# Two groups of rows finished inside the attention's first three steps, their rows kept in the weights' landing buffer

## The reference

```python
x = L0_attn_hidden_states                                   # [2, 2048, 256]
x = x + _layernorm(_L0_attn_ref(_layernorm(x), ...))        # part 1: local, compressed and selected attention
x = x + _layernorm(_L0_ffn_ref(_layernorm(x), ...))         # part 2: two transformer layers

# part 1, the end of it (win: 64 rows to a window, half overlapping)
combined = concatenate([comp_out * gates[..., 0:1], sel_out * gates[..., 1:2], win_out * gates[..., 2:3]], -1)
out = combined @ Wo + bo
out = out * 0.5 + hidden_states * 0.5
mu, var = out.mean(-1), out.var(-1)
return (out - mu) * rsqrt(var + 1e-06)

# part 2, one layer: x [2, 2048, 256]; 8 heads of 64; windows of 128 rows that look one window back
h = shift_token(x)                       # second half of the columns comes from the row before
q, k, v = split(h @ wqkv, 3)             # then l2norm, scales, rotary embedding
o = local_attention(q, k, v)
x = x + o @ wo
h = layernorm(shift_token(x)) * lg + lb
a, g = split(h @ w1 + b1, 2)
x = x + (a * gelu(g)) @ w2 + b2
```

## Time and profile before

| | |
|---|---|
| time, median of 3 runs | 1545.32 us (1541.97 to 1547.23) |
| the profiled execution | 1544.35 us, of which the span is 1542.2 us |
| instructions | 35890 |
| busy share: PE, DVE, ACT, POOL | 93%, 75%, 68%, 51% |
| the local stage's last matmuls end | at about 248 us |
| attention of layer 0 | about 261 to 680 us |

### The profile page before, as it was taken

One profiled execution on the slowest core, in us unless ns is written; L12 is line 12 of the kernel. 1 busy time (PEld: TensorE's weight loads), 2 busy tenths in 40 slices (PEclk: granted clock), 3 DMA queues, 4 the chain that ended last, 5 costly groups with the idle time before them and its releaser, 6 DMA issues.

```text
span 1542.2 us, 35890 instructions
## 1 busy us (share of the span) xinstructions
PE 1433.8 (93%) x10499; PEld 1195.9 (78%) x10499; DVE 1151.2 (75%) x3067; ACT 1047.3 (68%) x2678; POOL 791.9 (51%) x971
## 2 busy tenths in 40 slices
PE   8899995899999999959999979999999996899996
PEld 6458883688888888857888868888888885687775
DVE  6763686888888888856556488888888886656564
ACT  4222576788888888854545468888888886355553
POOL 4003266666666666623323556666666663334442
PEclk9999997999999999989999999999999998899998
DMA  5000323200000000002000020000000000111211
GB/s 182 1 1 18 136 94 113 59 7 6 5 5 7 5 5 5 5 8 94 16 23 16 19 66 6 7 5 5 5 5 5 5 5 8 32 37 32 63 33 60
DMA packets 59314, 46.63 MB, mean 30 GB/s; under 512 B 13662, under 2 KB 56002, under 8 KB 59234
## 3 DMA queue, kind: packets, MB, share of 16 engines
q1 hardware_dynamic: 59234, 45.65, 10.0%
HBM read 26.24 MB, written 8.39 MB: 22 GB/s over the span
## 4 chain that ended last, share of the span: by engine, by line
PE 76%; DVE 9%; ACT 6%; issue 4%; POOL 2%; DMA 1%; DVEq 0%; SPq 0%; ACTq 0%; POOLq 0%
PE bank L1993 8%; PE bank L2033 8%; PE bank L1934 7%; PE bank L1952 6%; PE bank L1855 6%; PE bank L1857 6%; PE bank L1856 6%; PE bank L1881 4%; PE bank L2107 3%; PE bank L2108 3%; PE bank L2109 3%; PE bank L1708 2%; DVE act_full L2813 2%; PE bank L1784 1%; PE bank L1717 1%
## 5 line engine op out<-in xcount | busy, mean ns | idle before, releaser
L1286 ACT ACTIVATE prob<-prob,neg_max 128x256 f32<-128x256 f32 x512 | 255.6, 507 | 1.2 <-DVE neg_max L2609 1.1
L850 POOL TENSOR_TENSOR rnorm<-sumsq,neg_half 128x8 f32<-128x8 f32 x128 | 213.5, 1668 | 23.4 <-POOL sumsq L847 22.7
L861 POOL TENSOR_TENSOR qk_cs<-qk_cs 128x512 f32<-128x512 f32 x128 | 181.7, 1420 | 56.0 <-DVE qk_cs L2489 55.7
L1855 PE MATMUL bank<-wqkv_hi,hT_hi 128*128 128x512 f32 x384 | 164.4, 428 | 19.3 <-DVE hT_lo L2471 19.3
L2489 DVE TENSOR_TENSOR qk_cs<-bank,rope 128x1024 f32<-128x1024 f32 x128 | 156.0, 1219 | 0.6 <-ACT qk_sq L1208 0.6
L2107 PE MATMUL bank<-h_hi,w_hi 128*128 128x512 f32 (+1 forms) x352 | 140.8, 400 | 14.5 <-POOL h_lo L909 14.4
L1856 PE MATMUL bank<-wqkv_lo,hT_hi 128*128 128x512 f32 x384 | 152.6, 397 | 0.0
L1857 PE MATMUL bank<-wqkv_hi,hT_lo 128*128 128x512 f32 x384 | 152.5, 397 | 0.0
L1439 ACT ACTIVATE act_hi<-act_full 128x512 fp32r<-128x512 f32 x96 | 60.7, 632 | 135.2 <-DVE act_full L2813 135.2
L1993 PE MATMUL bank<-ident,prob 128*128 128x128 f32 x1024 | 139.5, 280 | 5.1 <-DVE x_sb L2663 4.5
L2813 DVE SCALAR_TENSOR_TENSOR act_full<-bank,b_sb,gelu_sb 128x512 f32<-128x512 f32 x96 | 71.7, 746 | 93.1 <-ACT gelu_sb L1433 58.3
(11 more groups left out here) (291 smaller groups left out, 4166.8 us busy)
## 6 DMA issues: line engine op xcount, KB each, us to landing
x_sb<-in_L_attn_hidden_states SPq DMA_DIRECT2D x8, 512.0 KB, 7.6
x_in<-in_L_attn_hidden_states SPq DMA_DIRECT2D x8, 512.0 KB, 4.9
x_scratch<-x_in SPq DMA_DIRECT2D x8, 512.0 KB, 3.1
f_x<-x_scratch SPq DMA_DIRECT2D x8, 512.0 KB, 4.7
out<-f_y SPq DMA_DIRECT2D x8, 512.0 KB, 3.2
raw<-in_L_ffn_w SPq DMA_DIRECT2D x6, 640.0 KB
hs<-x_sb SPq DMA_DIRECT2D x16, 224.0 KB
hs<-x_sb SPq DMA_DIRECT2D x64, 56.0 KB
```

The lines of the kernel that those rows point to most:

```text
L850: pool.tensor_tensor(rnorm[:, part * HEADS:(part + 1) * HEADS], sumsq[:, which * HEADS:(which + 1) * HEADS], neg_half[:, 0:HEADS], ALU.pow ...
L861: pool.tensor_tensor(z, z, other[:, :, ::-1, :], ALU.add).then_inc(z_ready[which], 1)
L1286: act.activation(prob[:, h], prob[:, h], ACT.Exp, bias=neg_max[:, h:h + 1], scale=-1.0, accum_out=psums[:, h:h + 1]).then_inc(exped, 1)
L1855: pe.matmul(bank[:, to], hT_hi[:, c], wqkv_hi[:, c, cols], start=(c == 0), stop=False)
```

## The change

Groups 6 and 7 no longer use `x0_in`. Their rows are loaded into the first 2048 columns of `raw`, under the new name `x0_late`, after `ffn_split` has reached `FIRST`; `x0_of(g)` picks the place. The small tiles `f_bst1`, `f_mv1`, `f_r`, `f_shift` move out of the bytes that the attention uses. With that, the last part of the chain of groups 6 and 7 moves into the attention's steps, and ACT and DVE wait only for groups 0 to 5 before the first squares:

```diff
+        x0_late = raw[:].rearrange("p a n -> p (a n)")[:, 0:2 * GB * D].rearrange("p (a b d) -> p a b d", a=2, b=GB)
...
+        def x0_of(g):
+
+            return x0_late[:, g - (NG - 2)] if g >= NG - 2 else x0_in[:, g % 4]
...
                 sp.wait_ge(x1_stored, 16 * (g - 1))
-                sp.dma_start(x0_in[:, g % 4], group_of(x0_b, g)).then_inc(x0_loaded[g % 4], 16)
+                if g >= NG - 2:
+                    sp.wait_ge(ffn_split, FIRST)
+                    settle(sp)
+                sp.dma_start(x0_of(g), group_of(x0_b, g)).then_inc(x0_loaded[g % 4], 16)
...
@@ POOL: the local loop @@
-            for G in range(1, NG + 3):
+            for G in range(1, NG + 1):
...
@@ POOL: the attention's steps @@
                 for n in range(6):
                     step(n, n % 2)
+                    if not lay and n == 1:
+                        x1_scales(NG - 2)
+                        x1_scales(NG - 1)
...
             def first_hi():

                 act.wait_ge(hT_ps, 1)
                 act.wait_ge(x1_stored, 16 * 5)
+                act.wait_ge(x_made, GB * 5)
...
@@ ACT: the local loop @@
-            for n in range(NB + 18):
+            for n in range(NB + 6):
...
-                if n == NB + 12:
-                    first_hi()
                 if r < 2 and 0 <= n - 16 < NB:
                     b = (n - 16) // GB * GB + 2 * r
                     norm_x1(b)
                     norm_x1(b + 1)
+                if n == NB + 1:
+                    first_hi()
...
-                    act.wait_ge(x_made, NB)
-                    act.wait_ge(x1_stored, 16 * NG)
+                    act.wait_ge(x_made, NB - 2 * GB)
+                    act.wait_ge(x1_stored, 16 * (NG - 2))
...
@@ ACT: step 1, before kT, kT_lo and v_sb are cleared @@
+                    else:
+                        act.wait_ge(x1_made, NG)
...
@@ ACT: the attention's steps @@
                 for n in range(6):
                     step(n, n % 2)
+                    if not lay and n in (1, 2):
+                        for b in range(NB + (n - 3) * GB, NB + (n - 2) * GB):
+                            norm_x1(b)
...
@@ DVE: the local loop @@
-            for n in range(NB + 18):
+            for n in range(NB + 4):
...
@@ DVE: step 1, ahead of k_lo @@
+                        if type(n) is int and n == 1:
+                            if lay:
+                                add_up(lay * NG - 1, NG - 1)
+                            else:
+                                for b in range(NB - GB, NB):
+                                    x1_moments(b)
+                                    x1_aggregate(b)
...
                 if not lay:
                     lo(0, ahead=True)
-                    dve.wait_ge(x_made, NB)
-                    dve.wait_ge(x1_stored, 16 * NG)
+                    make_x1(NG - 1)
+                    x1_moments(NB - GB - 1)
+                    x1_aggregate(NB - GB - 1)
+                    dve.wait_ge(x_made, NB - 2 * GB)
+                    dve.wait_ge(x1_stored, 16 * (NG - 2))
```

More of the change, by code:

```diff
@@ L173, in build @@
         n_shift = place("n_shift", [P, GB])
+        f_bst1 = place("f_bst1", [P, 2, 6])
+        f_mv1 = place("f_mv1", [P, 2, GB, 2])
+        f_r = place("f_r", [P, 2, GB])
+        f_shift = place("f_shift", [P, 2, GB])
         base[0] = work_base
@@ L206, in build @@
         m_shift = place("m_shift", [P, 2, GB])
-        f_bst1 = place("f_bst1", [P, 2, 6])
-        f_mv1 = place("f_mv1", [P, 2, GB, 2])
-        f_r = place("f_r", [P, 2, GB])
-        f_shift = place("f_shift", [P, 2, GB])
+        place("spare", [P, 44])
         kTw = place("kTw", [P, 2, DC, UT])
@@ L554, in store_x1 @@
                     settle(sp)
-                sp.dma_start(group_of(x1_dram, g), x0_in[:, g % 4]).then_inc(x1_stored, 16)
+                sp.dma_start(group_of(x1_dram, g), x0_of(g)).then_inc(x1_stored, 16)
             def move_group(g):
@@ L759, in make_x1 @@
                 pool.wait_ge(x0_loaded[g % 4], LOCAL_X0 + 16 * (g // 4 + 1))
-                pool.tensor_tensor(x0_in[:, g % 4], x0_in[:, g % 4], xs_st[:], ALU.add).then_inc(x1_made, 1)
+                pool.tensor_tensor(x0_of(g), x0_of(g), xs_st[:], ALU.add).then_inc(x1_made, 1)
             def x1_scales(g):
@@ L1131, in norm_x1 @@
                 act.wait_ge(x1_root, g + 1)
-                act.activation(x_sb[:, b, :], x0_in[:, g % 4, r], ACT.Identity, bias=f_shift[:, g % 2, r:r + 1],
+                act.activation(x_sb[:, b, :], x0_of(g)[:, r], ACT.Identity, bias=f_shift[:, g % 2, r:r + 1],
                                scale=f_r[:, g % 2, r:r + 1]).then_inc(x_made, 1)
@@ L2405, in make_x1 @@
                 dve.wait_ge(x0_loaded[g % 4], LOCAL_X0 + 16 * (g // 4 + 1))
-                dve.tensor_tensor(x0_in[:, g % 4], x0_in[:, g % 4], xs_st[:], ALU.add).then_inc(x1_made, 1)
+                dve.tensor_tensor(x0_of(g), x0_of(g), xs_st[:], ALU.add).then_inc(x1_made, 1)
             def x1_moments(b):
                 dve.wait_ge(x1_made, b // GB + 1)
-                dve.bn_stats(f_bst1[:, b % 2], x0_in[:, b // GB % 4, b % GB]).then_inc(x1_stats, 1)
+                dve.bn_stats(f_bst1[:, b % 2], x0_of(b // GB)[:, b % GB]).then_inc(x1_stats, 1)
             def x1_aggregate(b):
@@ L2688, in step @@
                     if live(n, 1):
-                        if type(n) is int and n == 1 and lay:
-                            add_up(lay * NG - 1, NG - 1)
+                        if type(n) is int and n == 1:
[5 more added lines that the diff above has]
+                                    x1_aggregate(b)
                         k_lo(n - 1, 1 - i)
```

## The result

| | before | after |
|---|---|---|
| median, us | 1543.41 (1541.86 to 1547.48, 15 runs) | 1536.57 (1534.88 to 1541.97, 15 runs) |
| ratio, 95% interval | | 0.9956 (0.9947 to 0.9965) |
| profiled execution, us | 1544.35 | 1536.27 |
| its span, us; mean granted clock | 1542.2; 0.968 | 1534.2; 0.973 |

The kernel is 0.44% faster: 6.8 us between the medians, 8.1 between the profiled executions, 7.1 forecast.

What follows compares the result with a forecast made beforehand. PE bounds almost everywhere, but idled 13.24 us entering layer 0's attention, where ACT's order ended last. Terms -8.7 + 0.4 + 1.2 = -7.1 us gave 1537.25 from the profiled 1544.35, 1538.2 from the median; forecast 1537.5, range 1533.8 to 1542.2.

Steps and rivals of the forecast that it cites:

- Start of the projection: PE's first projection in layer 0's attention starts at about 251.2 us, 9.8 us earlier.
- First term: Entry to layer 0's attention: first squares and their sum come earlier, held by group 5's norms on ACT; -8.7 us.
- Second term: Four moment pairs on DVE in step 1, mostly inside old waits, delay PE's second projection; +0.4 us.
- Third term: ACT's four norms behind step 2 delay `qT` of block 1 and the square after it; +1.2 us.
- Costs taken as nothing: Moved POOL, ACT and SP work and later FFN weights cost nothing, with 0.5 to 0.6 us spare on ACT and POOL.
- Rival 1: Moved pieces on DVE and ACT cost their full 6.3 us, so the gain is 2.4 us: 1542.0; chance 0.17.
- Rival 3 and 4: 3: another dated wait holds the attention, 1544, chance 0.05. 4: repeated steps slow by 1.05 us, 1564.5, chance 0.04.
- Rival 2: PE's clock at the attention's entry returns sooner, 2.6 us less: 1534.7; or 1 to 2 us more; chance 0.12.
- both low stretches: PE's half-clock stretches at the first projection and from step 1's transposes stay unchanged, gaps being 3.4 and 3.7 us.

Runs made afterwards that it cites:

- early_pe: The kernel before with only `hT_hi` and `hT_lo` of block 0 brought forward, all norms still ahead of the squares; 1542.33 us, ratio 0.9991.
- only_group7: The changed kernel with group 6's scales and norms back ahead of the first squares, group 7's left in the attention; 1542.84 us, ratio 0.9990.
- pairs_apart: The changed kernel with group 7's four moment pairs split, two ahead of `normalise_k`, two behind block 1's `hT_lo`, and its POOL scales later; 1538.20 us, ratio 0.9958.
- norm7_in_gap: The changed kernel with group 7's norms on ACT moved from behind step 2 to between its squares of k and q; 1537.43 us, ratio 0.9948.
- filled: The changed kernel with 18 matmuls of unused product added on PE ahead of step 1's transposes; 1538.56 us, ratio 0.9962.
- pairs_filled: The changed kernel with the edits of both pairs_apart and filled; 1534.37 us, ratio 0.9943.
- best_again: pairs_filled run again unchanged, beside the changed kernel on the same chip; 1534.88 us, ratio 0.9939 to the kernel before.

## Why the prediction was right

The time (1537.5 forecast, 1536.57 measured), the direction and the order of the terms came out. By its own steps, with 2.30 us added to the times of after:

- *Start of the projection*, 251.2 forecast: 251.19. early_pe shows that the rest of the argument holds as well: PE's idleness was not what the gain hangs on.
- *First term*: first square 255.3 forecast, 255.37 measured; first `sumsq` 256.1 forecast, 256.10 measured. The decision that carried it was to take group 5's norms on ACT, not PE, as what ends last. only_group7 prices a group's norms there.
- *Second term*, +0.4: +0.30, and pairs_apart takes 0.33 back. `hT_lo` of block 1 was released by DVE's own work, as forecast.
- *Third term*, +1.2: +1.12, and norm7_in_gap takes 1.09 back. The scores of block 1 came at 281.43 (281.1 forecast), behind 1.05 us of idleness that `qT_lo` ended.
- *Costs taken as nothing* (POOL's scales, ACT's norms in step 1, SP's wait for `ffn_split`, the FFN weights 15 us later): PE and the masks wait for none of them in the rows of steps 1 to 3. DVE's `qT_lo` does wait for ACT's norms, and is done 0.5 us before the scores, the spare that was forecast. POOL's root ended at 269.47 (269.5 forecast, which is 278.2 less 8.7) and the masks came at 270.45, behind PE's scores. That cover is thin: in filled and only_group7 the masks did wait for the root, 0.51 and 0.63 us.
- *Rival 1*, full prices: fell, since the covers were there. *Rival 3 and 4*: no other wait, and 12.43 us per step in both layers.
- *Rival 2*, the clock: its half of gain did not come, the half of loss that it named did ("if the slow clock lasts into step 1's scores"), with 0.48 us. Since the kernel before has the same half clock over the scores in its second trace, the 0.48 can't be called a cost of the change.

The step that failed is the clock's: "So I carry both low stretches over as they are." The first stretch was shorter (3.5 us after PE resumed, not 6.1), the second lasted over the scores, and two of three traces have a third in step 2. The reason given, that both gaps stay longer than 2.58 us, does not carry: the kernel before itself, run again, kept full clock behind 3.40 us. The miss is 0.48 us in the forecast's trace and up to 2.1 with step 2's stretch in the two others; the sum of -7.1 came out as -6.8 in the first trace and as -5.5 in the mean of all.

So the three terms were right by their mechanism, each at its own place, and the closeness of the total is partly luck: the local stage's end and the rest of the span scatter by more (245.75 to 250.40, and 895.2 to 899.6) than the 0.9 us between forecast and median.

## What to carry to other kernels

Where a stage's last units delay the next stage's first ones, ask for each unit what stands ahead of the next stage's first instruction on every in-order engine: here PE's earlier start was worth 1.7 of 8.7 us, one group's norms 2.1, the other's with its wait 4.9. Count against it what the moved work costs inside the next stage: that was about 2 us for group 7, so moving it alone gained next to nothing, and only both groups together paid. Put moved work into a wait that the trace shows: the norms one place earlier gave 1.1 us, in two versions of the kernel. If two chains end within a microsecond of each other, change both in one experiment: neither edit alone moved the median, both together made the fastest version measured (pairs_filled and best_again, 0.9943 and 0.9939; with the norms in the gap 0.9940).
